# A graph network kernel on one core: the softmax over all edges with two work blocks in flight, the maximum subtracted by block, unrolled loops, and results stored block by block

## What is computed

```
alpha = jnp.where(alpha >= 0, alpha, 0.2 * alpha)           # one score per edge and head, 8 heads
amax  = jax.ops.segment_max(alpha, dst, num_segments=n)     # largest score of each destination
ex    = jnp.exp(alpha - amax[dst])
denom = jax.ops.segment_sum(ex, dst, num_segments=n)
attn  = ex / jnp.maximum(denom[dst], 1e-10)
out   = jax.ops.segment_sum(h_src * attn[..., None], dst, num_segments=n)
```

## Time and profile before

| | us |
|---|---|
| median of 3 runs | 6701.82 (6699.92 to 6706.92) |
| the profiled execution | 6704.29 |
| its span | 6702.5 |
| softmax stage in it, from the first instruction of L994 to the next stage | 4297.9 to 4498.1 |
| PE busy over the span | 5232.6 (78%) |
| DVE busy over the span | 3958.7 (59%) |
| ACT busy over the span | 1597.0 (24%) |
| POOL busy over the span | 3601.0 (54%) |

### The profile page before, as it was taken

How to read it: one execution, slowest core, us unless ns; L and a number is a source line. 1 busy time by engine, 2 the same in 40 slices (tenths; PEclk the granted TensorE clock), 3 DMA queues, 4 the chain that set the end, 5 groups by cost and what they waited for, 6 DMA issues and landing times.

```text
span 6702.5 us, 77622 instructions
## 1 busy us (share of the span) xinstructions
PE 5232.6 (78%) x19175; PEld 3659.0 (55%) x19176; DVE 3958.7 (59%) x9469; ACT 1597.0 (24%) x3103; POOL 3601.0 (54%) x3549
## 2 busy tenths in 40 slices
PE   5988886999998777777666666519999998777776
PEld 3777774777777433333344444306777876333333
DVE  4444445666664666666666666567766665555555
ACT  2444443444444000000122222212333332000000
POOL 0000003777775777777677777503333333777776
PEclk8999998999999777777788888659999998666666
DMA  5888886666665444444677777416767675444443
GB/s 201 321 315 321 313 321 231 218 215 215 218 214 205 122 124 123 124 124 123 198 241 245 242 244 244 155 57 217 236 235 238 230 241 177 117 116 117 116 116 111
DMA packets 467591, 1330.89 MB, mean 199 GB/s; under 512 B 136962, under 2 KB 261740, under 8 KB 409893
## 3 DMA queue, kind: packets, MB, share of 16 engines
q1 hardware_dynamic: 306773, 883.65, 37.1%
q0 software_dynamic: 160464, 443.17, 23.0%
HBM read 688.06 MB, written 638.42 MB: 198 GB/s over the span
## 4 chain that ended last, share of the span: by engine, by line
PE 54%; DMA 13%; DVE 11%; issue 9%; POOL 5%; SPq 4%; ACT 2%; DVEq 1%; ACTq 0%; POOLq 0%
PE ps L1399 26%; PE ps L1573 10%; PE ps L1423 8%; DMA table<-A 7%; PE ps L1556 5%; DMA work<-place_dram 3%; POOL A L629 2%; POOL ring L629 2%; SPq L366 2%; DVE W L814 2%; DVE A L814 2%; DMA xb_dram<-W 2%; PE ps L1378 1%; SPq L476 1%; PE ps L1363 1%
## 5 line engine op out<-in xcount | busy, mean ns | idle before, releaser
L617 POOL DMA_INDIRECT ring<-table,idx x2490 | 2370.3, 952 | 1908.1 <-DVEq L838 1045.7
L1399 PE MATMUL ps<-ring,W 128*128 128x256 f32 x3320 | 1207.2, 482 | 421.0 <-DVE W L814 260.4
L1399 PEld LDWEIGHTS ps<-ring,W 128*128 128x128 f32 x3320 | 685.7, 230 | 864.0 <-issue 411.9
L814 DVE TENSOR_SCALAR W<-iota,dloc,norm 128x128 f32<-128x128 f32 x1660 | 596.9, 360 | 773.6 <-PE ps L1399 763.4
L1399 PE MATMUL ps<-ring,A 128*128 128x256 f32 x1660 | 722.5, 542 | 273.7 <-DVE A L814 220.1
L642 POOL TENSOR_TENSOR ring<-ring,work 128x1024 f32<-128x1024 f32 x208 | 404.9, 1948 | 878.2 <-DMA ring<-rows_dram 878.2
L1573 PE MATMUL ps<-W_r,work_r 128*128 128x512 f32 x1960 | 701.1, 440 | 0.0
L832 DVE TENSOR_TENSOR X<-X,ps 128x256 f32 x1660 | 685.2, 413 | 13.0 <-PE ps L1399 10.6
L1399 PEld LDWEIGHTS ps<-ring,A 128*128 128x128 f32 x1660 | 341.1, 248 | 621.8 <-DVE A L814 381.2
L1378 PE MATMUL ps<-ring_r,work_r 128*128 128x512 f32 x1568 | 556.8, 407 | 109.1 <-DVE A_r L761 68.8
L1423 PE MATMUL ps<-W_r,work_r 128*128 128x512 f32 x1568 | 560.8, 440 | 0.0
(11 more groups left out here) (239 smaller groups left out, 7267.4 us busy)
## 6 DMA issues: line engine op xcount, KB each, us to landing
table<-A SPq DMA_DIRECT2D x98, 2048.0 KB, 9.4
ring<-rows_dram SPq DMA_DIRECT2D x208, 528.0 KB, 4.6
table<-A SPq DMA_DIRECT2D x98, 1024.0 KB, 4.6
table<-A SPq DMA_DIRECT2D x49, 1280.0 KB, 5.4
table<-W SPq DMA_DIRECT2D x49, 1280.0 KB, 7.0
rows_dram<-ring SPq DMA_DIRECT2D x52, 1056.0 KB, 4.7
rows_dram<-A SPq DMA_DIRECT2D x52, 1056.0 KB, 4.6
xb_dram<-W SPq DMA_DIRECT2D x49, 1024.0 KB, 3.9
```

Source lines behind the costliest of these rows:

```text
L617: pool.indirect_dma_start(out=f_ring[:, s % NR, :], out_offset=None, in_=src, in_offset=bass.IndirectOffsetOnAxis(ap=idx[:, s:s + 1], axis ...
L814: return dve.tensor_scalar(marks_[:, k % G, :], iota[:, :], dloc[:, k:k + 1], norm[:, k:k + 1], ALU.is_equal, ALU.mult).then_inc(wk.onehot ...
L1399: pe.matmul(ps[:, s % banks, 0:D], marks_[:, s % G, :], f_ring[:, s % NR, :], start=True, stop=True).then_inc(wk.step_done, 1)
```

## The change

The three loops are unrolled, with constants in the waits, and QB = 13 names the number of blocks. In detail:

- Turn in: `work` holds two blocks (scores and keys of block i at column `i % 2 * 1024`), and PSUM banks 0, 1 and 2, 3 are used in turn. DVE waits for the transposes of block i-2, and PE for the copies out of block i-2.
- Turn back: the subtraction of the maximum is cut in 13 pieces of 512 columns; DVE does two ahead, then piece i+2 before it takes block i out. The exp of block i waits for piece i and for the transposes of block i-2; it writes one of two halves of `work`. PE writes bank 2 or 3 and waits for the copy out of block i-2. The four copies of a block to the edge places are one instruction of 512 columns.
- The table load of exp: in the loop the compiler put one ahead of every exp; in unrolled code one is enough.
- Store: each block is stored by a DMA of its own (256 KB) when it is out. `ex_dram` is laid out as partition, block, q, 32 columns, and the reads of the sum stage follow that order; each still reads 32 numbers in a row per partition.

```diff
-    ex_dram = nc.dram_tensor("ex_dram", (P, NSC), F32).ap()
+    ex_dram = nc.dram_tensor("ex_dram", (P, QM // BLK, QS, BLK * HEADS), F32).ap()
...
             def keep_ex(_):
-                sp.wait_ge(m_out, QM // BLK + 1)
-                load(ex_dram, W[:, NSC:2 * NSC])
-                sp.wait_ge(loaded, seen[0])
+                for i in range(QB):
+                    sp.wait_ge(m_out, i + 1)
+                    sp.dma_start(ex_dram[:, i].rearrange("p q c -> p (q c)"), W[:, NSC + i * 512:NSC + (i + 1) * 512]).then_inc(m_kept, 16)
+                sp.wait_ge(m_kept, 16 * QB)
...
-                    sp.dma_start(s_ex[:, c % 4], ex_dram[:, c * CH * HEADS:(c + 1) * CH * HEADS].rearrange("p (k h) -> p k h", h=HEADS)
+                    sp.dma_start(s_ex[:, c % 4], ex_dram[:, c % QB, c // QB, :].rearrange("p (k h) -> p k h", h=HEADS)
...
# DVE, turn in
-                with dve.Fori(0, QM // BLK) as i:
-
-                    dve.wait_ge(m_turned, i + 1)
+                for i in range(QB):
+                    u = i % 2
+                    if i >= 2:
+                        dve.wait_ge(m_turned, i - 1)
                     for b in range(BLK):
-                        dst = work[:, b * P:(b + 1) * P].rearrange("p (q h) -> p q h", h=HEADS)
-                        key = work[:, 512 + b * P:512 + (b + 1) * P].rearrange("p (q h) -> p q h", h=HEADS)
-                        dve.tensor_copy(dst, av[:, :, bass.ds(i * BLK + b, 1), :].squeeze(2))
-                        ins = dve.tensor_copy(key, dv[:, :, bass.ds(i * BLK + b, 1)].to_broadcast([P, QS, HEADS]))
+                        dst = work[:, u * 1024 + b * P:u * 1024 + (b + 1) * P].rearrange("p (q h) -> p q h", h=HEADS)
+                        key = work[:, u * 1024 + 512 + b * P:u * 1024 + 512 + (b + 1) * P].rearrange("p (q h) -> p q h", h=HEADS)
+                        dve.tensor_copy(dst, av[:, :, i * BLK + b, :])
+                        ins = dve.tensor_copy(key, dv[:, :, i * BLK + b:i * BLK + b + 1].to_broadcast([P, QS, HEADS]))
                     ins.then_inc(m_copied, 1)
...
# DVE, turn back
-                ch(dve.tensor_tensor(alphaT, alphaT, maxT, ALU.subtract))
...
-                with dve.Fori(0, QM // BLK) as i:
-
-                    dve.wait_ge(m_back, i + 2)
-                    for b in range(BLK):
-                        ins = dve.tensor_copy(exq[:, :, bass.ds(i * BLK + b, 1), :].squeeze(2),
-                                              ps[:, 2, b * P:(b + 1) * P].rearrange("p (q h) -> p q h", h=HEADS))
-                    ins.then_inc(m_out, 1)
+                def below_max(i):
+                    part_ = slice(i * 512, (i + 1) * 512)
+                    dve.tensor_tensor(alphaT[:, part_], alphaT[:, part_], maxT[:, part_], ALU.subtract).then_inc(m_below, 1)
+
+                for i in range(2):
+                    below_max(i)
+                for i in range(QB):
+                    if i + 2 < QB:
+                        below_max(i + 2)
+                    dve.wait_ge(m_back, i + 1)
+                    dve.wait_ge(m_below, i + 1)
+                    dve.tensor_copy(W[:, NSC + i * 512:NSC + (i + 1) * 512].rearrange("p (q b h) -> p b q h", q=QS, h=HEADS),
+                                    ps[:, 2 + i % 2, :].rearrange("p (b q h) -> p b q h", b=BLK, h=HEADS)).then_inc(m_out, 1)
...
# ACT
+                for i in range(QB):
+                    act.wait_ge(m_turned, i + 1)
+                    act.activation(W[:, i * 512:(i + 1) * 512], ps[:, 2 * (i % 2), :], ACT.Copy).then_inc(m_evac, 1)
+                    act.activation(W[:, NSC + i * 512:NSC + (i + 1) * 512], ps[:, 2 * (i % 2) + 1, :], ACT.Copy).then_inc(m_evac, 1)
+                for i in range(QB):
+                    act.wait_ge(m_below, i + 1)
+                    if i >= 2:
+                        act.wait_ge(m_back, i - 1)
+                    act.activation(work[:, i % 2 * 512:(i % 2 + 1) * 512], W[:, i * 512:(i + 1) * 512], ACT.Exp).then_inc(m_exp, 1)
...
# PE, turn in
+                for i in range(QB):
+                    u = i % 2
                     pe.wait_ge(m_copied, i + 1)
+                    if i >= 2:
+                        pe.wait_ge(m_evac, 2 * (i - 1))
                     for b in range(BLK):
+                        pe.transpose(ps[:, 2 * u, b * P:(b + 1) * P], work[:, u * 1024 + b * P:u * 1024 + (b + 1) * P], ident[:, :])
+                    for b in range(BLK):
+                        ins = pe.transpose(ps[:, 2 * u + 1, b * P:(b + 1) * P], work[:, u * 1024 + 512 + b * P:u * 1024 + 512 + (b + 1) * P], ident[:, :])
                     ins.then_inc(m_turned, 1)
...
# PE, turn back
+                for i in range(QB):
                     pe.wait_ge(m_exp, i + 1)
+                    if i >= 2:
+                        pe.wait_ge(m_out, i - 1)
                     for b in range(BLK):
+                        ins = pe.transpose(ps[:, 2 + i % 2, b * P:(b + 1) * P], work[:, i % 2 * 512 + b * P:i % 2 * 512 + (b + 1) * P], ident[:, :])
                     ins.then_inc(m_back, 1)
```

More of the change, by code:

```diff
@@ L158, in build @@
         s_raw = [u[:, 0:1024].rearrange("p (c n) -> p c n", c=2) for u in s_unit]
-        assert KP % CH == 0 and WS + WS // 4 <= 2 * NSC and S_BANKS % 2 == 0
+        assert KP % CH == 0 and BLK == CH and WS + WS // 4 <= 2 * NSC and S_BANKS % 2 == 0
         NR = U
@@ L281, in build @@
         a_spill = [sem(f"a_spill{h}") for h in range(RH)]
-        m_copied, m_turned, m_evac, m_exp, m_back, m_out, m_cols, m_row = (sem("m_" + n) for n in (
-            "copied", "turned", "evac", "exp", "back", "out", "cols", "row"))
+        m_copied, m_turned, m_evac, m_below, m_exp, m_back, m_out, m_cols, m_row, m_kept = (sem("m_" + n) for n in (
+            "copied", "turned", "evac", "below", "exp", "back", "out", "cols", "row", "kept"))
+        QB = QM // BLK
         s_row = [sem(f"s_row{c}") for c in range(U // CH)]
@@ L994, in softmax @@
                 ch(dve.scalar_tensor_tensor(A[:, 0:NSC], A[:, 0:NSC], 0.2, A[:, 0:NSC], ALU.mult, ALU.max))
-                dve.sem_inc(m_turned, 1)
                 av = A[:, 0:NSC].rearrange("p (q m h) -> p q m h", q=QS, h=HEADS)
                 dv = dloc[:, 0:KP].rearrange("p (q m) -> p q m", q=QS)
-                with dve.Fori(0, QM // BLK) as i:
-                    dve.wait_ge(m_turned, i + 1)
+                for i in range(QB):
+                    u = i % 2
+                    if i >= 2:
+                        dve.wait_ge(m_turned, i - 1)
                     for b in range(BLK):
-                        dst = work[:, b * P:(b + 1) * P].rearrange("p (q h) -> p q h", h=HEADS)
-                        key = work[:, 512 + b * P:512 + (b + 1) * P].rearrange("p (q h) -> p q h", h=HEADS)
-                        dve.tensor_copy(dst, av[:, :, bass.ds(i * BLK + b, 1), :].squeeze(2))
-                        ins = dve.tensor_copy(key, dv[:, :, bass.ds(i * BLK + b, 1)].to_broadcast([P, QS, HEADS]))
+                        dst = work[:, u * 1024 + b * P:u * 1024 + (b + 1) * P].rearrange("p (q h) -> p q h", h=HEADS)
+                        key = work[:, u * 1024 + 512 + b * P:u * 1024 + 512 + (b + 1) * P].rearrange("p (q h) -> p q h", h=HEADS)
+                        dve.tensor_copy(dst, av[:, :, i * BLK + b, :])
+                        ins = dve.tensor_copy(key, dv[:, :, i * BLK + b:i * BLK + b + 1].to_broadcast([P, QS, HEADS]))
                     ins.then_inc(m_copied, 1)
-                dve.wait_ge(m_evac, 2 * (QM // BLK) + 2)
+                dve.wait_ge(m_evac, 2 * QB)
                 ch(dve.tensor_tensor(penalty[:, 1:NSC], keyT[:, 1:NSC], keyT[:, 0:NSC - 1], ALU.not_equal))
@@ L1067, in softmax @@
                 ch(dve.tensor_tensor_scan(maxT[:, ::-1], penalty[:, 1:NSC + 1][:, ::-1], prefix[:, ::-1], col[:, 6:7], ALU.add, ALU.max))
-                ch(dve.tensor_tensor(alphaT, alphaT, maxT, ALU.subtract))
-                dve.sem_inc(m_back, 1)
-                dve.sem_inc(m_out, 1)
-                exq = W[:, NSC:2 * NSC].rearrange("p (q m h) -> p q m h", q=QS, h=HEADS)
-                with dve.Fori(0, QM // BLK) as i:
-                    dve.wait_ge(m_back, i + 2)
-                    for b in range(BLK):
-                        ins = dve.tensor_copy(exq[:, :, bass.ds(i * BLK + b, 1), :].squeeze(2),
-                                              ps[:, 2, b * P:(b + 1) * P].rearrange("p (q h) -> p q h", h=HEADS))
-                    ins.then_inc(m_out, 1)
-                dve.wait_ge(m_out, QM // BLK + 1)
+                def below_max(i):
[10 more added lines that the diff above has]
+                                    ps[:, 2 + i % 2, :].rearrange("p (b q h) -> p b q h", b=BLK, h=HEADS)).then_inc(m_out, 1)
+                dve.wait_ge(m_out, QB)
             def attention_sum(_):
@@ L1516, in softmax @@
             def softmax(_):
-                with pe.Fori(0, QM // BLK) as i:
+                for i in range(QB):
+                    u = i % 2
```

(15 more changed lines are left out.)

## The result

| | before | after |
|---|---|---|
| median of 4 runs, us | 6702.83 (6699.92 to 6706.92) | 6641.26 (6636.84 to 6643.11) |
| ratio | | 0.9907, 95% interval 0.989 to 0.9924 |
| profiled execution | 6704.29 | 6636.84 |
| softmax stage in it | 200.2 | 133.1 |

The forecast was 6637.8 with a range of 6628 to 6654. The stage has four parts, read from the timelines as starts and ends on DVE: the turn in (from the slope instruction to the first comparison of keys), the scans, the turn back (from the end of the last scan to the end of the last copy) and the rest of the store.

What follows compares the result with a forecast made beforehand. The prediction saw no full engine but a relay in which one works and the others wait. Turn in 25.0, turn back 31.8 and store 7.2 sum to 64.0 less, from 6701.82 to 6637.8 us; range 6628 to 6654.

Steps and rivals of the forecast that it cites:

- The turn in: Softmax stage, slope instruction to first key comparison: 25.0 us less, ends 20 and 27.
- The step that carried the choice: Turn in: PE's clock rises from 0.50 without pauses, gain 25.0 us; rival that it stays, 28%, gain 20.6.
- The loop over two blocks: Turn in, PE and DVE: at the raised clock 2.49 us, or 1.25 per block, sets the pace.
- The 0.214 per transpose at half clock: Turn in, PE: each transpose takes 0.214 us at clock 0.50, so eight take 1.71.
- The turn back: Softmax stage, last scan's end to last copy's end: 49.9 us becomes 18.1, 31.8 less; ends 28 and 33.
- the load of the table: Turn back, ACT: one load stays, hidden during the scans at cost 0; rival of a load per exp, 3%, 8 us more.
- twelve loads: Turn back, ACT: removing twelve table loads is worth 15.4 us by the measured row, 32 by the skill's rule.
- The drain: Turn back, ACT: the skill's about 1380 ns per table change was forecast not to be in the block's period.
- The store: End of the softmax stage: stores by block leave 2.1 us instead of 9.28, 7.2 less; ends 5.4 and 7.6.
- Unrolled code: Rival, 10%: new instructions on the softmax stage's relay cost 6 us, giving 6644.
- The order of ex_dram: Sum stage reads: forecast 0; rival, 3%, that the new order makes them late and the kernel slower, 6721 us.
- The sum: Whole kernel: 25.0 + 31.8 + 7.2 = 64.0 us less.

Runs made afterwards that it cites:

- e9: The changed kernel once more, unedited: median 6635.01 us, ratio 0.9897 to the kernel before; softmax stage 134.2 us.
- e5: The changed kernel with POOL's clear of X moved behind the copies of the turn in: turn in 26.8 us, scans 86.0, softmax stage 132.1.
- e2: The changed kernel with one buffer in the turn in (waits for block i-1), still unrolled: turn in 53.9 us, softmax stage 157.8.
- e1: The kernel before with only the three loops of the turn back unrolled: turn back 35.8 us, softmax stage 186.0.
- e7: The changed kernel with ex_dram in its old order, so blocks are stored in 128-byte pieces: store 11.5 us, softmax stage 143.1.
- e8: The changed kernel with POOL's clear moved beside the first scan and 56 PE transposes ahead of the turn in: median 6630.04 us, stage 128.8.

## Why the prediction was right

- **The turn in** was forecast at 25.0 less and gave 26.6. The step that carried the choice, that PE's clock would rise once PE no longer pauses, held: it rose in the third block, 3.4 us after PE's first transpose (5.1 in e9, 6.0 in e5), and in e2, with the pauses kept, it didn't. The size of a warm block was 1.18 and not 1.25. The loop over two blocks, which the prediction took as the bound, is the bound; it was worked out as 2.49 and is 2.36. The hand-offs were sized from the looped kernel, 0.15 and 0.13, and are 0.04 and 0.06; PE's eight transposes take 1.09, a little over the 1.03 allowed. The 0.214 per transpose at half clock isn't 1.55 / 7, which is 0.221, since the first step is longer; it is the spacing of the others, and eight in a stream took 1.71 as forecast. The trace agrees with the Trainium skill's sentence that activity releases the throttle (TensorE: Matmul & The Clock Gate, "What's actually happening"): 1.71 per block before the rise and 1.18 after.
- **The turn back** was forecast at 31.8 less and gave 33.1: the 0.06 per block that I had added for waits isn't there (1.20 per block, not 1.27), and the last two blocks took 1.5 instead of 2.0 behind the eleventh copy. The 33.1 lies at the high end that was kept for this part, 33; with the 17.2 of the other runs it is 32.7. That the load of the table would move ahead of its wait was right, at 4331.99. That twelve loads were worth 15.4 was not: in e1 they and the unrolling together gave 1.05 for each, because the copies that the load covered came out from under it. It made no difference to the sum, which went by DVE's pace. The drain that the Trainium skill adds to each change of table (ScalarE: Activation LUTs, "What ACT_TABLE_LOAD costs") isn't seen: the gaps beside a load are 0.11 and 0.01.
- **The store**: 2.0 to its landing for 2.1. **Unrolled code** cost nothing and gave 2.4 (e2). **The order of ex_dram** did nothing to the reads.
- **The sum** was 64.0, the stage 67.1. The forecast lies 3.5 under the median of the first comparison and 2.8 over that of e9, so runs of one kernel scatter by about what the sum was off. That the total came so near is in part luck: the stage gained 3.1 more than forecast, while the medians of the first comparison differ by only 61.6.

## What to carry to other kernels

A relay of engines through single buffers costs the sum of its steps. A second buffer brings it to the slowest of them, or to half of one buffer's round where that is longer (1.18 here, with copies of 1.09). First work out both, then ask whether TensorE stays at its low clock once it has no pauses. Taking a step out of a relay is worth no more than the distance to the next chain beside it (1.05 for a load of 1.28 here). A store by block pays only if the destination's order lets the block be written in long pieces, and small gains of a stage are read in the stage's own timeline, since they vanish in the scatter of totals.

## What the runs showed of the hardware that I had not expected

- POOL's clear holds up some instructions of DVE and not others: copies of 128 columns in SBUF took 3.5 to 3.9 us instead of 0.21 and ended with it, and the multiplication by a constant took 5.06 instead of 3.63. The slope instruction (7.09), the scan (14.03) and in e5 the comparison of two tiles (7.09, from 5022.64) took the same beside it as elsewhere.
- With the loops unrolled one engine follows the other sooner: 0.03 and 0.05 us between PE and DVE in e2 for 0.15 and 0.13 before, and 0.04 for 0.18 in e1.
- The 13 stores of 256 KB in pieces of 128 bytes ran at 144 GB/s in e7; the single store of 3328 KB ran at 363 GB/s in its window.
- Chips differ: the kernel before took 6702 us in the first comparison and beside e8 and e9, but 7546 and 7565 on the two chips of e1 to e7, with the same scans of 84.6 us in the softmax stage. The runs don't show whether that is the chips themselves or their state at the time.
